# Quantised cross attention: two of seven row tiles turned by DMA instead of by PE, turns one tile later, sums and clips moved to GpSimd

## The reference

```
def _fq(x, delta, zp, n_bits):
    xi = round(x / delta) + zp
    xq = clip(xi, 0, 2 ** n_bits - 1)
    return (xq - zp) * delta

q = x @ wq;  k = ctx @ wk;  v = ctx @ wv          # split into 16 heads of 8
sim  = einsum(fq(q, dq, 128, 8), fq(k, dk, 128, 8)) * SCALE
attn = softmax(sim, axis=-1)
out  = einsum(fq(attn, dw, 0, 8), fq(v, dv, 128, 8))
```

## Time and profile before

| | us |
|---|---|
| median of three runs | 2368.3 |
| the profiled execution | 2363.04 |
| its span, first to last instruction | 2361.1 |
| PE busy (20005 matmuls) | 1944.1 |
| DVE busy | 1692.9 |
| ACT busy | 1365.7 |
| GpSimd busy | 965.9 |

### The profile page before, as it was taken

How to read it: one execution, slowest core, us unless ns; L and a number is a source line. 1 busy time by engine, 2 the same in 40 slices (tenths; PEclk the granted TensorE clock), 3 DMA queues, 4 the chain that set the end, 5 groups by cost and what they waited for, 6 DMA issues and landing times. The chain is left out here.

```text
span 2361.1 us, 58647 instructions
## 1 busy us (share of the span) xinstructions
PE 1944.1 (82%) x20005; PEld 1289.1 (55%) x20005; DVE 1692.9 (72%) x3300; ACT 1365.7 (58%) x2415; POOL 965.9 (41%) x763
## 2 busy tenths in 40 slices
PE   4888676699999999999788875446888889888888
PEld 4878243266666666666435552223555555555553
DVE  4999496666666666666322347994999999999984
ACT  2454243366666666666333333224988888888863
POOL 2332151444544454444000003322776676666630
PEclk7999798799999999999888895557999999999989
DMA  7776000223333333333049940001111111101100
GB/s 198 243 245 215 5 1 0 79 80 93 90 92 84 92 90 91 85 92 77 1 140 288 280 128 0 0 0 40 41 40 39 39 39 39 38 27 39 39 1 16
DMA packets 64285, 190.36 MB, mean 81 GB/s; under 512 B 19886, under 2 KB 27294, under 8 KB 64222
## 3 DMA queue, kind: packets, MB, share of 16 engines
q1 hardware_dynamic: 59614, 164.95, 24.9%
q0 software_dynamic: 4608, 24.58, 2.7%
HBM read 127.13 MB, written 25.49 MB: 65 GB/s over the span
## 5 line engine op out<-in xcount | busy, mean ns | idle before, releaser
L1284 DVE TENSOR_REDUCE c_part<-c_mxp 128x1 f32<-128x500 f32 x672 | 428.6, 677 | 211.8 <-PE c_mxp L1164 211.6
L1232 ACT ACTIVATE c_e<-c_stp 125x896 f32<-125x896 f32 x384 | 349.3, 917 | 167.5 <-PE c_stp L1178 166.2
L1908 ACT ACTIVATE c_e<-c_sp,alpha 128x750 f32<-128x750 f32 x448 | 392.8, 882 | 23.1 <-PE c_sp L1852 20.8
L1866 PE MATMUL c_tp<-ident_h,c_ph 128*128 128x128 f16 x2688 | 229.4, 223 | 73.2 <-DVE c_pt L1928 71.2
L1866 PEld LDWEIGHTS c_tp<-ident_h,c_ph 128*128 128x128 f16 x2688 | 179.9, 100 | 168.2 <-DVE c_pt L1928 114.3
L1164 PE MATMUL c_mxp<-c_kh,c_qb 128*128 128x500 f16 x672 | 254.5, 381 | 7.1 <-DVE c_part L1284 3.7
L1822 POOL TENSOR_SCALAR c_ki<-c_clipped 128x500 bf16<-128x500 bf16 x96 | 193.0, 2010 | 150.2 <-DVE c_clipped L1939 140.9
L1928 DVE TENSOR_SCALAR c_pt<-c_tp 125x768 bf16<-125x768 f16 x448 | 246.1, 550 | 4.8 <-issue 2.7
L1972 DVE TENSOR_SCALAR c_ph<-c_e,c_inv 128x1500 f16<-128x1500 f32 x224 | 223.4, 997 | 4.3
L1852 PE MATMUL c_sp<-c_ki,c_qb 128*128 128x375 bf16 x896 | 223.0, 331 | 1.4 <-ACT c_e L1908 1.4
L1822 POOL TENSOR_SCALAR c_vi<-c_clipped 125x512 bf16<-125x512 bf16 x96 | 196.2, 2044 | 60.3 <-DVE c_clipped L1939 59.0
(11 more groups left out here) (275 smaller groups left out, 3652.6 us busy)
## 6 DMA issues: line engine op xcount, KB each, us to landing
c_ct<-ctx_turned SPq DMA_DIRECT2D x64, 750.0 KB
ctx_turned<-l_ct POOLq DMA_DIRECT2D x32, 750.0 KB, 4.2
c_ks<-c_kh SPq DMA_DIRECT2D x256, 93.8 KB
f_ct<-ctx_turned SPq DMA_DIRECT2D x32, 750.0 KB
l_cn<-in_ctx SPq DMA_DIRECT2D x32, 672.0 KB
f_cn<-in_ctx SPq DMA_DIRECT2D x32, 672.0 KB
c_ks<-c_kl SPq DMA_DIRECT2D x128, 93.8 KB
l_cn<-in_ctx SPq DMA_DIRECT2D x32, 78.0 KB
```

The lines of the kernel that those rows point to most:

```text
L1232: act.activation(e[:, j % (2 * GROUP), :].rearrange("p (a c) -> p a c", a=2), stp[0:KP, 2 * (j % 2):2 * (j % 2) + 2, 0:448], ACT.Exp, scal ...
L1284: dve.reduce_max(part[:, s // 3, s % 3:s % 3 + 1], mxp[:, (PIECES * p + s) % 2, 0:500], axis=AX.X).then_inc(piece_max, 1)
L1866: last = pe.transpose(tp[:, h, 128 * k:128 * k + 128], ph[r][:, KP * j:KP * j + 128], m.ident_h[:, :])
L1908: act.activation(e[r][:, HALF * h:HALF * h + HALF].rearrange("p (k c) -> p k c", k=2), sp_[:, 2 * h:2 * h + 2, 0:375], ACT.Exp, scale=m.al ...
```

## The change

Two of seven row tiles (1 and 4, `BY_DMA`) are turned by a DMA transpose issued on SP, from bf16 buffers `pc` that DVE clips first; the other five are turned by PE as before, all of them three tiles behind the scores (`TURN_LAG`). e and ph have four buffers each. Weights of tile t are made in the DVE slot of tile t + 1. The sum of the halves goes to GpSimd (`totalled`). Of the roundings, the three of V go from ACT to DVE; both clips of all six go to GpSimd, as two operations with two constants each on fp32, in place of one on DVE and one with a single constant on GpSimd. Projections stand at tiles 0, 1, 2, 4, 5, 6; the weighted sum at tiles 4 and 6. Keys lie in 12 blocks of 128, the last padded with zeros. The diff, cut to its core:

```
+        PROJECT = (0, 1, 2, 4, 5, 6)
+        WEIGH = {4: (0, 6), 6: (6, NJ)}
+        TURN_LAG = 3
+        E_BUFFERS = 4
+        ON_VECTOR = (3, 4, 5)
+        BY_DMA = (1, 4)
+        USED_BACK = [4 if t >= E_BUFFERS else NT if t == 3 else 3 for t in range(NT)]
...
             def _(sp):
+                sp.wait_ge(set_once, SETS)
                 def step(n, p, live):
+                    if live(0):
+                        if live(2):
+                            sp.wait_ge(proj_done, 6 * (n - 1))
+                        sp.dma_start(ct[p][:, 0:NK], ctx_turned[...]).then_inc(ctx_loaded[p], 16)
                     if live(2):
+                        a = n - 2
+                        if live(4):
+                            wait_apart(sp, weighed, NJ * (a - 1), beat)
+                        for k, t in enumerate(BY_DMA):
+                            wait_apart(sp, p_clipped, ND * a + k + 1, beat)
+                            sp.dma_start_transpose(pt[p][:, :, 128 * t:128 * t + 128], pc[k][:, :]
+                                                   ).then_inc(dma_turned[k], 16)
...
             def _(pool):
+                def clip(n, p, k, live):
+                    if k >= 2 or live(1):
+                        pool.wait_ge(proj_ready, i - 1)
+                    wait_apart(pool, proj_rounded, i + 1, beat)
+                    pool.tensor_scalar(clamped[k % 2][...], rounded[k % 2][...],
+                                       ROUND + 127.0, ROUND - 128.0, ALU.min, ALU.max).then_inc(proj_clamped, 1)
+                    if k < 3 and live(2):
+                        pool.wait_ge(s_done, 2 * NT * (n - 1))
+                    if k >= 3 and live(2):
+                        pool.wait_ge(weighed, NJ * (n - 2) + 4 * (k - 2))
+                    wait_apart(pool, proj_clamped, i + 1, beat)
+                    pool.tensor_scalar(out, clamped[k % 2][...], -ROUND, 1.0, ALU.add, ALU.mult
+                                       ).then_inc(proj_ready, 1)
                 def step(n, p, live):
                     (the head spread of batch n first, as before)
+                    for t in range(NT):
+                        if live(1):
+                            wait_apart(pool, exped, 2 * i + 2, beat)
+                            pool.tensor_scalar(total[:, t:t + 1], half[:, t, 0:1], half[:, t, 1:2], m.delta[:, 7:8],
+                                               ALU.add, ALU.mult).then_inc(totalled, 1)
+                        if live(0) and t in PROJECT:
+                            clip(n, p, PROJECT.index(t), live)
...
             def _(dve):
+                def weights(a, t, first):
+                    dve.wait_ge(inverted, i + 1)
+                    (waits until ph of four tiles back is turned or clipped)
+                    dve.tensor_scalar(ph[t % E_BUFFERS][:, 0:NK], e[t % E_BUFFERS][:, :], inv[:, t:t + 1],
+                                      HALF_ROUND, ALU.mult, ALU.add).then_inc(p_ready, 1)
+                    if t in BY_DMA:
+                        dve.wait_ge(p_ready, i + 1)
+                        if not first:
+                            dve.wait_ge(dma_turned[k], 16 * a)
+                        dve.tensor_scalar(pc[k][:, 0:NK], ph[t % E_BUFFERS][:, 0:NK], HALF_ROUND + 255.0,
+                                          HALF_ROUND, ALU.min, ALU.subtract).then_inc(p_clipped, 1)
                 per tile t: copies of tile t - 3 (none for tiles 1 and 4), reciprocal and weights of tile t - 1,
+                        if live(0) and t in PROJECT and PROJECT.index(t) in ON_VECTOR:
+                            dve.wait_ge(proj_done, i + 1)
+                            dve.wait_ge(proj_clamped, i - 1)
+                            dve.tensor_scalar(rounded[k % 2][0:128, :], pp[0:128, 0:512], m.rdelta[0:128, 6:7],
+                                              ROUND, ALU.mult, ALU.add).then_inc(proj_rounded, 1)
```

More of the change, by code:

```diff
@@ L1759, in quantised_cross_attention @@
         pair = lambda name, shape, d=F32: [sb(f"{name}{p}", shape, d) for p in range(2)]
-        W = NK + 4
+        W = 128 * NJ
         HALF = NK // 2
-        WEIGH = [0, 2, 5, 7, 9, NJ]
-        ct = pair("ct", [128, NK])
+        PROJECT = (0, 1, 2, 4, 5, 6)
[4 more added lines that the diff above has]
+        BY_DMA = (1, 4)
+        BY_PE = [t for t in range(NT) if t not in BY_DMA]
+        ND, NP = len(BY_DMA), len(BY_PE)
+        USED_BACK = [4 if t >= E_BUFFERS else NT if t == 3 else 3 for t in range(NT)]
+        ct = pair("ct", [128, W])
         ki = pair("ki", [128, NK], BF16)
-        vi = pair("vi", [KP, NJ, D], BF16)
+        vi = pair("vi", [128, NJ, D], BF16)
         rounded = pair("rounded", [128, 512])
-        clipped = pair("clipped", [128, 512], BF16)
+        clamped = pair("clamped", [128, 512])
         qb = pair("qb", [128, HQ], BF16)
[L1769 to L1773, removed]
+        e = [sb(f"e{t}", [128, NK]) for t in range(E_BUFFERS)]
+        ph = [sb(f"ph{t}", [128, W], F16) for t in range(E_BUFFERS)]
+        pc = [sb(f"pc{k}", [128, W], BF16) for k in range(ND)]
+        half = sb("half", [128, NT, 2])
+        total, inv = sb("total", [128, NT]), sb("inv", [128, NT])
+        pt = pair("pt", [128, NJ, HQ], BF16)
         masked = sb("masked", [128, 4, NQ])
@@ L1824, in _ @@
-                sweep(pool, step, 0)
+                    pool.memset(ct[p][:, NK:W], 0.0).then_inc(set_once, 1)
+                for t in range(E_BUFFERS):
+                    pool.memset(ph[t][:, NK:W], 0.0).then_inc(set_once, 1)
+                for k in range(ND):
+                    pool.memset(pc[k][:, NK:W], 0.0).then_inc(set_once, 1)
+                def clip(n, p, k, live):
+                    i = 6 * n + k
+                    rows, width = (128, 500) if k < 3 else (128, 512)
+                    if k >= 2 or live(1):
+                        pool.wait_ge(proj_ready, i - 1)
+                    wait_apart(pool, proj_rounded, i + 1, beat)
+                    pool.tensor_scalar(clamped[k % 2][0:rows, 0:width], rounded[k % 2][0:rows, 0:width],
+                                       ROUND + 127.0, ROUND - 128.0, ALU.min, ALU.max).then_inc(proj_clamped, 1)
[4 more added lines that the diff above has]
+                    wait_apart(pool, proj_clamped, i + 1, beat)
+                    out = (ki[p][:, 500 * k:500 * k + 500] if k < 3 else
+                           vi[p][:, 4 * (k - 3):4 * (k - 3) + 4, :].rearrange("p j c -> p (j c)"))
+                    pool.tensor_scalar(out, clamped[k % 2][0:rows, 0:width], -ROUND, 1.0, ALU.add, ALU.mult
+                                       ).then_inc(proj_ready, 1)
@@ L1951, in step @@
                                     dve.wait_ge(weighed, NJ * (n - 2))
-                                copy_turned(n - 1, 1 - p, t - 2, h)
-                            if h == 0 and live(1):
-                                dve.wait_ge(exped, 2 * i + 2)
-                                if t or live(2):
-                                    dve.wait_ge(inverted, i)
-                                dve.scalar_tensor_tensor(out=total[:, :], in0=half[:, r, 0:1],
-                                                         scalar=half[:, r, 1:2], in1=m.delta[:, 7:8],
-                                                         op0=ALU.add, op1=ALU.mult).then_inc(summed, 1)
```

171 lines of the change are left out of this document (87 added, 84 removed).

## The result

The changed kernel took 2345.4 us (median of 4 runs, 2337.2 to 2346.5) against 2368.0 for the kernel before on the same chip (4 runs), ratio 0.990, 95% interval [0.987, 0.993]. So it is faster, by 22.6 us where 48 were forecast. The profiled execution has a span of 2344.8 us for 2361.1, which is less of a difference, because the one before lay 5 us under its median. From its first load to the last scaling the stage took 656.0 us (1625.40 to 2281.44) for 676.6 (1620.37 to 2296.96). Before, the first memset started with that load; now it starts at 1624.53 and the load waits for the memsets. So 0.9 us of the later start belongs to the change and 4.2 us to code that is the same, and from the first memset on the stage is 19.7 us shorter.

What follows compares the result with a forecast made beforehand. Bound: ACT and PE in the tiles, plus a batch-boundary stall from GpSimd shutting out DVE. A step was to fall from 20.36 to 18.6 us (16.0 + 2.4 + 0.2), 30 steps saving 53 us, ends adding 5: 2320 us, range 2255 to 2400.

Steps and rivals of the forecast that it cites:

- GpSimd, 10.3 us by itself: GpSimd's own work per batch, from 13.9 us: twelve clip operations at 0.6, seven totals at 0.2, head spread 1.68.
- rival 3: GpSimd too slow, from 0.5 us a total or 0.77 a clip operation on: 2400 us; chance 0.10.
- DVE, 14.6 us busy: DVE's work per batch: 18.9 us less 7.5 of sums, clips and copies, plus 3.2 of roundings and new clips.
- The coupling, 2.4 us on DVE: GpSimd and DVE shut each other out: 1.4 us from nine DVE operations, about 1.0 from the head spread, per batch.
- One more wait is added: At the batch boundary DVE's reciprocal waits for tile 0's total, queued behind GpSimd's head spread: 0.2 us a batch.
- The sum: 18.6 us a batch for 20.36 over 30 steps, 53 us less, 5 more at the ends: -48 us, 2320.
- The ends, + 5: Start and end of the stage: 2 us more for memsets before the first load, 3 for the last batch.
- DMA, no wait: SP's queue per batch: two transposes of 2.5 to 6 us and the load, at most 17 us in 18.6.
- rival 2: The DMA transposes are the bound, slower from 7.7 us each; at 9 us each 2449 us; chance 0.13.
- Rival 1: The lock costs nothing extra and PE's 16.4 us a batch is the bound: 2256 us; chance 0.13.
- Rival 4: The gain is eaten by DVE waiting in GpSimd's order, a step stays at 20.2 us: 2368 us; chance 0.06.
- end-to-end length of 18.4 us: Per batch, GpSimd's 10.3 us and DVE's SBUF operations (seven weights, two new clips) laid end to end under the lock.

Runs made afterwards that it cites:

- e15: Changed kernel with DVE's reciprocal reading the first half's sum, so it no longer waits for GpSimd's totals, which are still made: 2298.1 us, ratio 0.972.
- e14: Kernel before the change, with GpSimd's clip given two constants in place of one: 2364.1 us, ratio 0.998.
- e16: Changed kernel with V roundings on ACT, head spread after tile 4, clips one tile later, all seven tiles turned by PE: 2276.6 us, ratio 0.962.
- e13: Changed kernel with V roundings on ACT, head spread after tile 4 and each projection's clip one tile later: 2284.3 us, ratio 0.966.
- e5: Changed kernel with the totals moved back from GpSimd to DVE: 2354.0 us, ratio 0.995.

## Why the prediction came out as it did

The direction and the sources were right, the size was half. By its own steps:

- **ACT, 14.9 us, PE, 16.4 us**: measured 14.5 and 16.5.
- **GpSimd, 10.3 us by itself**: the first operation of a clip at 0.60 us as I took it. The second was taken at 0.6 too and is 1.23 for K and 0.86 for V behind weights; a total is 0.34 at the least and 0.42 in the mean for the 0.2 I took. Busy 15.1. By the mean over its twelve clip operations, (3 x 0.60 + 3 x 0.61 + 3 x 1.23 + 3 x 0.86) / 12 = 0.83 us, rival 3's condition of 0.77 was met; its price of 2400 was not paid, since this stretching is the lock itself, which it counted a second time.
- **DVE, 14.6 us busy**: measured 16.7. The new operations took 2.2 + 1.6 us for 3.2, 0.6 more. The weights rose by 0.04 us each, 0.3. The largest piece is one of method: I took 7.5 us out by means of groups, and in these records neighbours on DVE overlap. Summed over all groups a step has 22.0 us before and 18.5 after, where busy is 19.0 and 16.7; the overlap shrank by 1.2. 14.6 + 0.6 + 0.3 + 1.2 = 16.7.
- **The coupling, 2.4 us on DVE**: the lock is there, but 0.3 us in the weights and 0.4 in the new clips (2 x (0.79 - 0.58)) is all that falls on DVE's own operations. The remainder fell on GpSimd's, 0.7 for the spread and about 0.6 for each K clip, and reached DVE as waits. The sign I had named for the lock, weights over 1.1 us in the mean, did not appear (1.03).
- **"One more wait is added: the total of tile 0 stands behind the head spread ... I add 0.2 us of it"**: this is the step that failed. That wait alone is 1.44 us, because the spread itself is held up by the weights (2.37 us for 1.68), and two more that the prediction did not have (0.83, 0.36) make 2.63 us a step. e15 takes the waiting away and leaves all of GpSimd's work, and the step falls from 19.77 to 18.12 us, the time by 47 us.
- **The sum**: in place of 16.0 + 2.4 + 0.2 = 18.6 it reads 16.7 + 0.4 + 2.63 = 19.77. Against the forecast that is 2.4 more of waits, 1.0 less of gaps (0.4 for the 1.4 in the 16.0, though my own terms add to 1.6) and 0.3 less of busy time. That DVE's busy time with its lock came so near (17.0 forecast, 16.7) is luck: 1.4 too little work and 1.7 too much lock cancel. 30 x (20.38 - 19.77) = 18 us.
- **The ends, + 5**: from the first memset on the stage shortened by 19.7 us, 18.3 of them in the steps, so the ends gave 1.4 us and cost nothing. The memsets overlap one another (1624.53 to 1625.37), and the first load left 0.9 us after the first of them, where I added 2 us.
- **DMA, no wait**: right, and rival 2 is out. **Rival 1**, 2256: out. **Rival 4** forecast 20.2 a step, by DVE waiting for totals and roundings in GpSimd's order; its mechanism is the one that decided, and it gave a step 0.4 us too long.
- **Not in the prediction**: that the slow third steps at clock 0.92 end. Against full-clock steps the change gained 0.2 us, and 0.4 of the 0.6 is the clock. What ended it is open: it stayed at 1.00 in e14 too, with PE busy 17.4 of 20.18 us, and in e16 with 16.8 of 17.59.

The prediction weighed the end-to-end length of 18.4 us as a floor. e13 refutes this. From its single durations GpSimd has 7 x 0.34 + 12 x 0.61 + 1.69 = 11.4 us and DVE's SBUF operations 7 x 0.98 + 2 x 0.58 = 8.0; together 19.4, in a step of 17.75. Its timeline shows how:

```profile
1857.04 0.37 DVE L2035 TENSOR_TENSOR c_masked<-c_op,mask_quad_ 128x224 f32<-128x224 f32 x1
...
1858.20 0.62 POOL L1845 TENSOR_SCALAR c_vi<-c_clamped 128x512 bf16<-128x512 f32 x1 [0.18 <-issue]
...
1858.21 1.40 DVE L1992 TENSOR_SCALAR c_ph<-c_e,c_inv 128x1500 f16<-128x1500 f32 x1
...
1860.52 0.98 DVE L1992 TENSOR_SCALAR c_ph<-c_e,c_inv 128x1500 f16<-128x1500 f32 x1
...
1860.70 1.29 POOL L1845 TENSOR_SCALAR c_vi<-c_clamped 128x512 bf16<-128x512 f32 x1 [0.18 <-issue]
```

The weights at 1858.21 end at 1859.61, 0.79 us after the clip beside them, where alone they take 0.98. The clip at 1860.70 ends 0.49 us after the weights do, where alone it takes 0.62. So each such meeting leaves 0.13 to 0.2 us side by side. Over the 26 steps of the stretch 16 pairs meet in a step, with 2.4 us side by side by these single durations, and for 0.8 us of a step neither works: 19.4 - 2.4 + 0.8 = 17.8. The Trainium skill, SBUF — State Buffer, section "SBUF: two separate sides", has the lock held for the whole instruction. The rows agree except for these 0.13 to 0.2 us, and except for the short DVE operations beside bf16 clips in the last section.

The Trainium skill, VectorE: DVE Perf Modes, section "The three transpose paths", has 1309 ns for one block by DMA. As a rate it would have made 31 us a batch (320 us slower in all by 30 x (31 - 20.36), and over 400, as I wrote, only with the load's 4.9 us in each step); the step of 19.77 with no wait for a transpose shows that it is none.

## What to carry to other kernels

When work moves from a busy engine to one that it shares a port with, price the waits that come back: list, for each value that returns to the first engine, what stands ahead of it in the second's queue at its longest duration beside the first engine's work, not at its shortest. Take busy time out by what a stretch's busy sum falls, since group means of neighbouring operations overlap. And test the edits of a bundle one by one: here one of them (V rounding on DVE) cost about 50 us, more than twice what the bundle gained, and another (DMA transposes) gave nothing.

## What the runs showed of the hardware

- A GpSimd operation with two constants on 500 to 512 columns took 0.60 us from fp32 to fp32. From bf16 to bf16 it took 1.87 us with two constants (e14) and 1.45 with one, where DVE did nothing beside it, and 2.62 and 2.03 in the median.
- Beside a bf16 clip the lock holds only in part. In e14:

```profile
1759.45 2.62 POOL L1822 TENSOR_SCALAR c_ki<-c_clipped 128x500 bf16<-128x500 bf16 x1 [2.44 <-DVE c_clipped L1939]
...
1760.56 0.20 DVE L1958 SCALAR_TENSOR_TENSOR c_total<-c_half,delta 128x1 f32<-128x1 f32 x1
...
1761.22 0.40 DVE L1939 TENSOR_SCALAR c_clipped<-c_rounded 128x500 bf16<-128x500 f32 x1
1761.54 1.33 DVE L1972 TENSOR_SCALAR c_ph<-c_e,c_inv 128x1500 f16<-128x1500 f32 x1
```

  The weights that start inside the clip end 0.80 us after it (1762.87 for 1762.07), just as behind a head spread; so they look shut out to its end. But a sum of 0.20 us and a clip of 0.40 start and end inside it, unstretched, where in e5 the same sum inside an fp32 operation of 0.61 us took 0.42 and ended with it (1703.45). What decides which DVE operation has to wait was not tried.
- A one-column operation on GpSimd takes 0.34 us, more than half of one on 500 columns, and 1.02 us where it starts beside weights (1858.81 in e13).
- DVE's clip of 1500 columns from fp16 to bf16 takes 0.57 to 0.58 us when nothing meets it.
